# The router's query in components, four weight pieces read from staging, and an earlier start for the low halves of two probability tiles, in a fused FFN, attention, FFN layer

## The reference

```python
x = x + 0.5 * ffn(layernorm(x))
x = x + attn(layernorm(x))          # 32 query heads, 8 key/value groups, head size 128, rotary, causal softmax
x = x + 0.5 * ffn(layernorm(x))
# in ffn, h is its input:
query = h @ Wq.T                                  # 64 wide
scores = (query @ Wr.T) @ (keys @ Wr.T).T / sqrt(48) + log_rel     # 128 slots
attn   = query @ keys.T / sqrt(64) + log_rel      # softmax over the 8 slots of the highest scores
aux    = softmax8(attn) @ values @ Wvd.T @ Wvu.T
out    = h + gate(h) * aux                        # the gate from a gelu layer and the token's variance
```

## Time and profile before

| | us |
|---|---|
| median of 3 runs (lowest to highest) | 1443.12 (1442.22 to 1446.02) |
| profiled execution, its own time | 1443.21 |
| its span, first to last instruction | 1441.4 |
| PE busy | 1371.9 (95%) |
| DVE busy | 1191.1 (83%) |
| ACT busy | 950.9 (66%) |
| POOL busy | 702.1 (49%) |

### The profile page before, as it was taken

The page is one execution under the profiler, slowest core; times in us unless marked ns, Lnnn a source line. Parts: engine busy times, 40 slices in busy tenths (PEclk is TensorE's granted clock), DMA queues, the critical chain, the costliest instruction groups (busy, mean ns, idle before and its releaser), DMA issues.

```text
span 1441.4 us, 26246 instructions
## 1 busy us (share of the span) xinstructions
PE 1371.9 (95%) x8686; PEld 777.5 (54%) x8816; DVE 1191.1 (83%) x2869; ACT 950.9 (66%) x2452; POOL 702.1 (49%) x593
## 2 busy tenths in 40 slices
PE   5778999998999999999999999999999999999996
PEld 3445555554555655555555655555555555555553
DVE  6798978899898888988878888889877798777657
ACT  4567777667677676656666677666666676666654
POOL 3177767667764344345545354434534454434321
PEclk9799999999999999999999999999999999999998
DMA  8376777779667576556657655557665677555443
GB/s 295 117 168 147 196 163 195 170 178 220 167 150 168 114 147 144 117 137 136 140 127 162 137 134 137 122 128 139 143 136 131 147 140 155 113 137 124 96 91 117
DMA packets 440278, 212.11 MB, mean 147 GB/s; under 512 B 382128, under 2 KB 383344, under 8 KB 440144
## 3 DMA queue, kind: packets, MB, share of 16 engines
q1 hardware_dynamic: 439024, 209.05, 63.0%
q10 hardware_dynamic: 1120, 1.38, 0.3%
HBM read 91.88 MB, written 25.17 MB: 81 GB/s over the span
## 4 chain that ended last, share of the span: by engine, by line
PE 74%; DVE 15%; issue 4%; ACT 3%; POOL 2%; DMA 1%; SPq 1%; DVEq 0%; ACTq 0%
PE PJ L1427 17%; PE PJ L1428 16%; PE PJ L1426 16%; DVE phl L1176 4%; PE PV L1426 4%; PE PV L1428 4%; PE PV L1427 4%; PE SC L1600 4%; PE SC L1602 4%; PE SC L1601 4%; DVE p L1166 2%; POOL t L592 2%; DVE t L1122 1%; DVE t L1120 1%; DVE t L1121 1%
## 5 line engine op out<-in xcount | busy, mean ns | idle before, releaser
L607 POOL TENSOR_TENSOR oTl<-of,oTf 128x512 f16<-128x512 f32 x128 | 154.7, 1209 | 457.7 <-ACT oTf L770 457.5
L778 ACT ACTIVATE p<-p,mn 128x512 f32<-128x512 f32 (+3 forms) x512 | 280.8, 549 | 97.2 <-DVE mn L1166 97.1
L1176 DVE SCALAR_TENSOR_TENSOR phl<-p,ri,phl 128x128 f16<-128x128 f32 (+3 forms) x512 | 339.3, 703 | 0.0
L1426 PE MATMUL PJ<-XT,wsp 128*128 128x512 f16 x640 | 243.6, 381 | 10.1 <-DMA wsp<-kept 6.9
L789 ACT ACTIVATE phl<-p,ri 128x128 f16<-128x128 f32 (+3 forms) x512 | 245.6, 550 | 4.1
L1427 PE MATMUL PJ<-XT,wsp 128*128 128x512 f16 x640 | 243.4, 380 | 0.0
L1428 PE MATMUL PJ<-XT,wsp 128*128 128x512 f16 x640 | 243.3, 380 | 0.0
L592 POOL TENSOR_TENSOR t<-t 128x512 f32<-128x512 f32 x158 | 202.2, 1280 | 66.3 <-DVE t L1122 66.0
L1166 DVE CUSTOM_DVE_ANT_0 p<-SC,maskw 128x512 f32<-128x512 f32 (+3 forms) x512 | 219.9, 485 | 3.1 <-issue 0.4
L1427 PE MATMUL PJ<-wosp,oTf 128*128 128x512 f16 x512 | 194.0, 379 | 4.4
L597 POOL TENSOR_TENSOR qTl<-t,qTh 128x512 f16<-128x512 f32 x127 | 147.9, 1165 | 92.5 <-ACT qTh L754 92.5
(11 more groups left out here) (237 smaller groups left out, 2621.9 us busy)
## 6 DMA issues: line engine op xcount, KB each, us to landing
wsp<-kept SPq DMA_DIRECT2D x150, 256.0 KB, 3.1
wosp<-kept SPq DMA_DIRECT2D x96, 256.0 KB, 3.3
raw<-in_wqkv SPq DMA_DIRECT2D x48, 256.0 KB, 4.6
kept<-wsp SPq DMA_DIRECT2D x42, 256.0 KB, 2.5
raw<-in_wo SPq DMA_DIRECT2D x32, 256.0 KB, 4.7
kept<-wosp SPq DMA_DIRECT2D x32, 256.0 KB, 3.3
pTf<-phl SPq DMA_TRANSPOSE x256, 3.8
X<-in_x SPq DMA_DIRECT2D x3, 1024.0 KB, 9.0
```

The costliest lines, as they stand in the source:

```text
L607: ins = nc.gpsimd.tensor_tensor(oTl[:, n % 2, h, c], of[:, s % 2, c], oTh[:, n % 2, h, c], ALU.subtract)
L778: ins = nc.scalar.activation(pt, pt, ACT.Exp, bias=mn[:, par, i:i + 1], scale=-1.0, accum_out=rs[:, par, i:i + 1])
L1176: nc.vector.scalar_tensor_tensor(out=phl[:, par, low(i, 0):low(i, i) + 1, :], in0=p[:, par, SOFF[i]:SOFF[i] + w].rearrange("p (k t) -> p k ...
L1426: mm(out_, lh, rh, start=start, stop=False)
```

## The change

1. **Query by components.** The setup no longer multiplies Wq into the keys. `wq2` holds Wq.T scaled by row (`fqr`, the reciprocal of a mean absolute value), in float16, its high half in columns 0 to 63 and the low in 64 to 127. `query(f, bb)` multiplies it with both halves of the normalized tokens: 4 chunks x 2 matmuls give the query's parts on 128 partitions, the high weights' in 0 to 63 and the low weights' in 64 to 127. ScalarE (`query_hi`) and VectorE (`query_lo`) split it into `qfh` and `qfl`, and `score_tiles` needs 3 matmuls of 256 columns for a tile, with `bh` and `bl`, the halves of [Wr.T rk, keys.T] on 128 partitions (both copies, scaled by `fqs`). For the first and the last sequence's FFN at the start and the end (`apart`) the query comes in two pieces of 256 columns.
2. **Tables.** QRY stands at u 6 and 15, the score tiles of the first FFN at 7 and 9 instead of 6 and 8; `qhi` and `qlo` on ScalarE and VectorE likewise. `RING` and `TAIL` have the new tasks in them, `QRT` being the second piece at the end.
3. **Staging.** Unit 1's K, Q0, Q1 and V are read by the projections where they were made (`FROM_STAGING`), and no longer loaded; GpSimd's `out_lo` of steps 0, 2, 4 and 6, which overwrites these buffers, waits for the projections.
4. **Values.** `attend` waits for turn 0, does the 8 products with high halves, waits for turn 1 and does the 4 with low halves.
5. **Low halves.** `p_lo(s, 0)` and `p_lo(s, 1)` stand at the end of step s on VectorE.

```diff
-PE_A = {6: [("SCR", 0, 0)], 8: [("SCR", 0, 1)], 10: [("HID", 0, 0)], 12: [("HOUT", 0, 0), ("ET", 0, 0)],
+PE_A = {6: [("QRY", 0, 0)], 7: [("SCR", 0, 0)], 9: [("SCR", 0, 1)], 10: [("HID", 0, 0)], 12: [("HOUT", 0, 0), ("ET", 0, 0)],
...
-PE_B = {16: [("SCR", 1, 0)], 22: [("SCR", 1, 1)], 28: [("HID", 1, 0)], 30: [("ET", 1, 0), ("HOUT", 1, 0)]}
+PE_B = {15: [("QRY", 1, 0)], 16: [("SCR", 1, 0)], 22: [("SCR", 1, 1)], 28: [("HID", 1, 0)], 30: [("ET", 1, 0), ("HOUT", 1, 0)]}
...
-        + [(("SCR", 1, 3, 0), 1), (("MEAN", 1, 0, 0), 0), (("HID", 1, 3, 0), 2), (("SCR", 1, 3, 1), 3),
-           (("SCT",) + APART, 0), (("HOUT", 1, 3, 0), 2)]
+        + [(("QRY", 1, 3, 0), 0), (("QRT", 1, 3, 1), 1), (("SCR", 1, 3, 0), 2), (("MEAN", 1, 0, 0), 0), (("SCR", 1, 3, 1), 3),
+           (("SCT",) + APART, 1), (("HID", 1, 3, 0), 0), (("HOUT", 1, 3, 0), 2)]
...
+FROM_STAGING = [(1, k) for k in PIECES[:4]]
...
-    out = [(1, "K"), (1, "Q0")] if s == 0 else []
+    out = []
...
-    return out + [(n + d, kind) for d, kind in REFILL[h] if 0 <= n + d < NU]
+    return out + [(n + d, kind) for d, kind in REFILL[h] if 0 <= n + d < NU and (n + d, kind) not in FROM_STAGING]
...
+                    pool.wait_ge(s_k, 2)
+                if s == 2:
+                    pool.wait_ge(s_q, 5)
+                if s == 4:
+                    pool.wait_ge(s_q, 6)
+                if s == 6:
+                    pool.wait_ge(s_v, 2)
...
+                k = QUERIES.index((f, bb))
+                if k and j == 0:
+                    f_, b_ = QUERIES[k - 1]
+                    act.wait_ge(r_sc[f_], 4 * b_ + 4)
+                c = query_columns(f, bb, j)
+                nc.scalar.copy(qfh[:, c], query_bank(f, bb, j)).then_inc(q_hi[f], 2 if apart(f, bb) else 4)
...
-            act.wait_ge(fs_pe, 1)
-            nc.scalar.copy(rk[:, :], PJ[0:RDIM, 3, 0:NSLOT]).then_inc(fs_ev, 1)
-            act.wait_ge(fs_pe, 2)
-            nc.scalar.copy(rmat, PJ[0:BOT, 2, 0:NSLOT]).then_inc(fs_ev, 1)
-            for c in range(CC):
-                act.wait_ge(fs_pe, 3 + c)
-                nc.scalar.copy(ah[:, c, :], setup_bank(c)).then_inc(fs_hi, 1)
+            act.wait_ge(fs_pe, prepared("pe", "rk"))
+            nc.scalar.copy(rk[:, :], SC[0:RDIM, 0, 0:NSLOT]).then_inc(fs_act, 1)
+            act.wait_ge(ld_fq, 16)
+            nc.scalar.activation(t1[:, 0, :], fwq, ACT.Abs, accum_out=fql[:, 0:1]).then_inc(fs_act, 1)
+            turned_hi(0, 0, 0)
+            act.wait_ge(fs_dve, prepared("dve", "wq scales"))
+            nc.scalar.activation(t1[0:BOT, 1, :], fwq[0:BOT, :], ACT.Copy, scale=fqr[0:BOT, 0:1]).then_inc(fs_act, 1)
+            turned_hi(0, 0, 1)
+            act.wait_ge(fs_pe, prepared("pe", "wqT"))
+            nc.scalar.copy(wq2[:, :, 0:BOT], SC[:, 2, 0:CC * BOT].rearrange("p (c d) -> p c d", c=CC)).then_inc(fs_act, 1)
+            turned_hi(0, 0, 2)
+            turned_hi(0, 0, 3)
+            act.wait_ge(fs_pe, prepared("pe", "rmat"))
+            nc.scalar.activation(bh[:, 0:NSLOT], SC[:, 1, 0:NSLOT], ACT.Copy, scale=fqs[:, 0:1]).then_inc(fs_act, 1)
+            nc.scalar.activation(bh[:, NSLOT:2 * NSLOT], fkeyT[:, :], ACT.Copy, scale=fqs[:, 0:1]).then_inc(fs_act, 1)
+            query_hi(0, 0, 0)
+            query_hi(0, 0, 1)
...
+            def query_lo(f, bb, j=0):
+                dve.wait_ge(q_hi[f], query_tiles(f, bb, j))
+                c = query_columns(f, bb, j)
+                nc.vector.tensor_tensor(qfl[:, c], query_bank(f, bb, j), qfh[:, c], ALU.subtract
+                                        ).then_inc(q_lo[f], 2 if apart(f, bb) else 4)
...
+            def query_factors():
+                dve.wait_ge(fs_act, prepared("act", "wq sums"))
+                link(nc.vector.tensor_scalar(fqs[:, :], fql[:, :], 1.0 / 256, 1e-30, ALU.mult, ALU.max))
+                nc.vector.reciprocal(fqr[:, :], fqs[:, :]).then_inc(fs_dve, 1)
+            def query_weights_lo():
+                dve.wait_ge(fs_act, prepared("act", "wq"))
+                nc.vector.tensor_tensor(wq2[:, :, BOT:2 * BOT], SC[:, 2, 0:CC * BOT].rearrange("p (c d) -> p c d", c=CC),
+                                        wq2[:, :, 0:BOT], ALU.subtract).then_inc(fs_dve, 1)
+            def score_weights_lo():
+                for k, whole in enumerate((SC[:, 1, 0:NSLOT], fkeyT[:, :])):
+                    c = slice(k * NSLOT, (k + 1) * NSLOT)
+                    dve.wait_ge(fs_act, prepared("act", f"b{k}"))
+                    nc.vector.scalar_tensor_tensor(out=bl[:, c], in0=whole, scalar=fqs[:, 0:1], in1=bh[:, c], op0=ALU.mult,
+                                                   op1=ALU.subtract).then_inc(fs_dve, 1)
...
-            for i in range(4):
-                normal(0, 0, i)
-            for c in range(CC):
-                setup_lo(c)
-            for i in range(4):
-                turned_lo(0, 0, i)
+            normal(0, 0, 0)
+            normal(0, 0, 1)
+            query_factors()
+            normal(0, 0, 2)
+            normal(0, 0, 3)
+            turned_lo(0, 0, 0)
+            turned_lo(0, 0, 1)
+            query_weights_lo()
+            turned_lo(0, 0, 2)
+            turned_lo(0, 0, 3)
+            score_weights_lo()
+            query_lo(0, 0, 0)
+            query_lo(0, 0, 1)
...
-                    p_lo(s - 1, 0)
-                    p_lo(s - 1, 1)
                     p_lo(s - 1, 2)
...
-            for k in range(TB):
+                p_lo(s, 0)
+                p_lo(s, 1)
+            for k in (2, 3):
                 p_lo(NS - 1, k)
...
+            def query(f, bb, j=0):
+                free(("QRT" if j else "QRY", f, bb, j))
+                hi, lo = xt_of(2 * f, bb)
+                for t in range(2 * j, 2 * j + 2) if apart(f, bb) else range(TB):
+                    turned(2 * f, bb, t)
+                cols = query_columns(f, bb, j)
+                for c in range(CC):
+                    mm(query_bank(f, bb, j), wq2[:, c, :], hi[:, c, cols], start=c == 0, stop=False)
+                    ins = mm(query_bank(f, bb, j), wq2[:, c, :], lo[:, c, cols], start=False, stop=c == CC - 1)
+                ins.then_inc(q_ps[f], 2 if apart(f, bb) else 4)
             def score_tiles(f, bb, j):
                 free(("SCR", f, bb, j))
-                hi, lo = xt_of(2 * f, bb)
+                pe.wait_ge(q_lo[f], query_tiles(f, bb, j))
                 for t in range(2):
-                    turned(2 * f, bb, 2 * j + t)
                     if (f, bb, 2 * j + t) == APART:
                         free(("SCT", f, bb, 2 * j + t))
-                    dst = score_bank(f, bb, 2 * j + t)
                     ts = lo_slice(2 * j + t)
-                    for c in range(CC):
-                        ins = mm3(dst, hi[:, c, ts], lo[:, c, ts], ah[:, c, :], al[:, c, :], c == 0, c == CC - 1)
-                    ins.then_inc(r_sc[f], 1)
+                    mm3(score_bank(f, bb, 2 * j + t), qfh[:, ts], qfl[:, ts], bh[:, :], bl[:, :], True, True
...
-                w = weight_slot(kind, n)
+                w = made_slot(kind, n) if (n, kind) in FROM_STAGING else weight_slot(kind, n)
...
-                for r in range(2):
-                    pe.wait_ge(p_turned[par][r], 16 * (s // 2) + 16)
+                pe.wait_ge(p_turned[par][0], 16 * (s // 2) + 16)
                 if h == 0:
                     pe.wait_ge(v_lo, n + 1)
                 if s:
                     pe.wait_ge(o_hi, s)
                 for j in range(TB):
                     hi = pT[:, par, high(j, j):high(TB - 1, j) + 1, :].rearrange("p k t -> p (k t)")
+                    mm(PV[:, j * P:T], vh[:, n % 2, j, :], hi, start=j == 0, stop=False)
+                    mm(PV[:, j * P:T], vl[:, n % 2, j, :], hi, start=False, stop=False)
+                pe.wait_ge(p_turned[par][1], 16 * (s // 2) + 16)
+                for j in range(TB):
                     lo = pT[:, par, low(j, j):low(TB - 1, j) + 1:3, :]
-                    ins = mm3(PV[:, j * P:T], vh[:, n % 2, j, :], vl[:, n % 2, j, :], hi, lo, j == 0, j == TB - 1)
+                    ins = mm(PV[:, j * P:T], vh[:, n % 2, j, :], lo, start=False, stop=j == TB - 1)
...
-            mm(PJ[0:RDIM, 3, 0:NSLOT], fwrT[:, :], fkeyT, start=True, stop=True).then_inc(fs_pe, 1)
-            pe.wait_ge(fs_ev, 1)
-            mm(PJ[0:BOT, 2, 0:NSLOT], fwr[:, :], rk[:, :], start=True, stop=True).then_inc(fs_pe, 1)
-            pe.wait_ge(ld_fq, 16)
-            pe.wait_ge(fs_ev, 2)
+            mm(SC[0:RDIM, 0, 0:NSLOT], fwrT[:, :], fkeyT[0:BOT, :], start=True, stop=True).then_inc(fs_pe, 1)
+            pe.wait_ge(fs_act, prepared("act", "rk"))
+            mm(SC[:, 1, 0:NSLOT], fwr[:, :], rk[:, :], start=True, stop=True).then_inc(fs_pe, 1)
+            pe.wait_ge(cst, 1)
+            ffn_task(HEAD[0])
+            ffn_task(HEAD[1])
+            pe.wait_ge(fs_act, prepared("act", "wq rows"))
             for c in range(CC):
-                mm(setup_bank(c), fwq[:, c * P:(c + 1) * P], rkey[:, :], start=True, stop=True).then_inc(fs_pe, 1)
```

(18 more changed lines are left out.)

128 lines of the change are left out of this document (79 added, 49 removed).

## The result

| | before | changed |
|---|---|---|
| median (lowest to highest), us | 1444.28 (1442.22 to 1446.02) | 1472.30 (1471.93 to 1472.83) |
| ratio of the times (95% interval) | | 1.0196 (1.0180 to 1.0212) |
| span of the profiled execution, us | 1441.4 | 1470.4 |
| PE / DVE busy, us | 1371.9 / 1191.1 | 1371.8 / 1211.1 |

The change is slower by 28 us, where 13 us faster was forecast. That PE's busy time looks unchanged, with 208 matmuls fewer, is no finding: the profile before holds 8686 matmul records beside 8816 weight loads, so some 130 matmuls are missing from it, and the one after holds 8604 of each.

What follows compares the result with a forecast made beforehand. TensorE alone was taken to bound 400 to 1400 us, with VectorE often late before. Terms -10.9 - 1.1 - 1.5 - 2.8 + 1.4 + 0.6 + 1.0 = -13.3 us from 1443.21 gave 1429.9 us, range 1418 to 1438.

Steps and rivals of the forecast that it cites:

- low halves 0 and 1 at the end of their step: VectorE, between minima and reciprocal: 0.7 us wait per step, hidden in the full stretch; two steps counted, +1.4 us (0 to +22).
- Scores in the full stretch: TensorE, 400 to 1400 us: fewer score matmuls save 2.2 us in each of five batches, counted whole, -10.9 us.
- -1.1 for scores: First pass's batch 1, 128 to 198 us: half the 2.2 us score saving counted, -1.1 us (0 to -2.2).
- high halves first: Value products before 400 us: eight of twelve matmuls no longer wait for the second turn, -2.8 us (0 to -10).
- staging: Early projections: the 6.9 us wait for weights from DRAM goes, but VectorE is nearly full, -1.5 us (0 to -6.9).
- Start: Setup before the first scores: 0.18 MB more loaded ahead of the constant gb, +0.6 us (0 to +2).
- end: Kernel's tail: logarithms now behind the query halves, gelu behind matmuls starting later, +1.0 us (-1 to +3).
- Rival 2: Before 400 us: the reciprocal's wait is paid in a dozen more steps, 8 us, giving 1438 us; chance 0.15.
- Rival 3: Every step: GpSimd blocks both moved low halves, VectorE bounds everywhere, 71 us more, 1512; decides from 1.2 us per step; chance 0.03.
- Rival 4: TensorE: saved matmuls turn into waits for query halves or banks, nothing to measure, 1440 us; chance 0.06.
- Rival 1: 58 to 400 us: early stages recover 10 us more of TensorE's idle time, giving 1420 us; chance 0.18.
- signs of being wrong: VectorE's minima over 7 us behind their bank after 400 us, TensorE waiting for query halves, stretch to step 32 not shorter.

Runs made afterwards that it cites:

- e1: Changed kernel with only the move of low halves 0 and 1 undone (behind the next step's minima again): 1436.84 us, ratio 0.9940.
- e3: Kernel before with only low halves 0 and 1 moved to the end of their step: 1465.47 us, ratio 1.0145.
- e12: Kernel before with low halves 0 and 1 moved and the 512-wide low half put ahead of the reciprocal: 1436.72 us, ratio 0.9948.
- e4: Changed kernel with the low-half move and the high-half-first value products both undone: 1434.49 us, ratio 0.9930.
- e9: Kernel before with only the query by components and its tables (tail logarithms in the new order): 1435.90 us, ratio 0.9952.
- e2: Changed kernel with the 512-wide low half put ahead of the reciprocal, filling the gap there: 1427.81 us, ratio 0.9884.
- e11: Changed kernel with the 512-wide low half ahead of the reciprocal and low halves 0 and 1 right behind Q's rotation: 1424.79 us, ratio 0.9871.
- e7: Changed kernel with low halves 0 and 1 ahead of Q's rotation, the gap ahead of the reciprocal left open: 1598.99 us, ratio 1.1071.

## Why the prediction was wrong

- **Failed: low halves 0 and 1 at the end of their step, +1.4 (0 to +22).** Measured: +35.5 (e1 against the change). The mechanism was right, and so was its size, "some 0.7 us in such a step": 0.79 in the trace, 99.3 us in all. Two steps of the argument fell. "In the full stretch that is 8.5 + 0.7 = 9.2 us of a step of 10.4, hidden": 1.2 us were taken as slack, from busy time, where the waits for TensorE, the only slack at the end of a step, were 10.2 us in 32 steps, 0.32 a step. And the upper bound of 22 us left out the 96 later steps on that ground, so the range, which ended at 1438, could not hold it. The longer low halves, which the term puts at nothing ("Their work is the same"), add to it: 6.8 us of busy time against 20.0 us of wait in sequence 1, and most of the 6.2 us of sequence 0. Without this term the sum has 14.7 us less than before; e1 has 7.6.
- **Scores in the full stretch, -10.9.** Right: 4.1 + 4.4 + 2.2 = 10.7 in sequences 1 to 3 (e1). In the changed kernel they show in the last sequence alone.
- **Sequence 0: -1.1 for scores, -2.8 for high halves first, -1.5 for staging.** Measured together in e1: +0.75. Staging was right (about 2). The other two were taken to be half on the path. VectorE's busy time and waits for ScalarE, 298.28 + 19.5 + 17.5 + 1.2, fill 336.5 of the 340.21 us of sequence 0 before, so what TensorE saved there turned into its own waiting.
- **Start +0.6, end +1.0.** The first selection now starts at 24.27, 2.6 us later than in the earlier trace rows, with a longer wait for gb (4.55), so the 0.6 was too small; how much of it reaches step 0 is not settled (-0.6 to +2.1 in the executions with part 1, while e3 and e12, without it, lie 1.5 below the profile of before). The end is 0.58 shorter in e1 and 0.05 and 0.24 longer in e4 and e9 (60.82, 61.45 and 61.64 against 61.40): less than the 1.0, with no clear sign.
- **The rivals.** Rival 2 had the mechanism and put it before 400 us only, 8 us for a dozen steps; the traces have it in 22 steps of sequence 0, without more waiting in sum, and in 31 of 32 in sequences 1 and 2, where it was paid. Rival 3 said what became of the kernel, VectorE as the bound, and overpriced the way to it: two blocked instructions per step, 71 us. Measured, the low halves' busy time grew by 27.0 us in all, and that of the two moved shapes by 29.6 (75.9 + 83.1 to 85.2 + 103.4). "It decides from 1.2 us lost per step" is the same false slack. Its price alone would not have decided: e2 carries 20.9 us of it and is fast, and e11 carries 117 and is no slower. Rival 4, that saved matmuls turn into waits, came true in sequence 0 alone. Rival 1 did not come. How much of the 28 us the clash is answerable for beside the wait was not separated; by the busy time it is at most 5.9 of the 27.4 us in the account of sequence 1, the query's work included; of what part 5 costs in sequence 0 it is the greater part.
- **What was to show it.** "ScalarE releases the reciprocal in most steps, with 0.7 us each" came true. "TensorE is still over 99% busy in the long stretch" did not: 97.4%. Of the signs of being wrong, two came clearly: VectorE's minima lie up to 9.56 us behind their bank after 400 us (2.88 before), and the stretch to step 32 is longer (417.83 against 409.32). The third, TensorE waiting for query halves, is 1.9 us in 2 waits. One count was off without touching the sum: the queries are 48 matmuls of 512 and 32 of 256 columns, 80 and not 64.

Beside rival 3 stood a rule of the Trainium skill (SBUF — State Buffer, "Who interferes with whom"). The runs agree with it as to the fact: the same low half, 128 by 256, takes 528 ns on average in e7 and 1291 in e11, where GpSimd is in its sum. The time that rival 3 drew from it did not come: once TensorE is the bound, as in e2 and e11, the clash is paid from VectorE's waits.

## What to carry to other kernels

Idle time of an engine is not yet slack. Sum its busy time and its waits for third engines for each repeating piece of the program, and compare that with the bound; a wait for a third engine is slack only for work that is put ahead of that very wait, as e11 does. Work between a producer and the instruction that waits for a third engine is cover; whoever takes it away must put something else there, and a swap of two instructions can be worth more than the change itself (44 us here). If work is moved to a new place, trace the circle it joins there: what it waits for, too, is now in front of everything behind it.

## What the runs showed that was not expected

The duration of one and the same VectorE instruction depends on its place by more than a factor of two (528 to 1291 ns on average for the 256-wide low half), while GpSimd's own operations beside it hardly change: its sum of rotated halves takes 1280 ns on average before, 1271 in the change and 1344 in e11. And the extra busy time need not cost anything: e11 has 96 us more of low halves than e2, and its median is 3.0 us lower. (Of its 47.5 us against the changed kernel, 44.5 are the filled gap's.)
